# A graph stage's element-wise steps go through PSUM, its bias edge to GpSimd, and its inputs get a second buffer

## What is computed

```
# graph block
Xw = X @ Wv + bv
e = leaky_relu(Xw @ aw[:d] (as a row) + Xw @ aw[d:] (as a column) + ab, 0.2)
alpha = A * exp(e);  transition = alpha / (row sum of alpha + 1e-12)
H = sum over k = 0..2 of Xk @ Wk[k] + bk[k],  with Xk = transition @ Xk from one k to the next
return relu(H)

# ffn block: fc1, then a Mamba layer, then fc2
u, z = split(h @ W_in.T);  u = silu(causal conv of 4 taps over u + conv_b)
dt, B, C = split(u @ W_xproj.T);  delta = softplus(dt @ W_dt.T + b_dt)
state = exp(delta * A) * state + (delta * u) * B      # 1024 channels x 16 states, along the 128 positions
y = sum over the 16 states of state * C + u * D;  y = y * silu(z)
return fc2(y @ W_out.T) + b_fc2
```

## Time and profile before

| | |
|---|---|
| median of three runs | 4198.68 us |
| the profiled execution | 4201.61 us, span 4199.6 us |
| VectorE busy | 3672.1 us (87%) |
| TensorE busy (weight loads beside it) | 3628.5 us (86%) (2059.3) |
| GpSimd busy | 3444.9 us (82%) |
| ScalarE busy | 2875.8 us (68%) |
| C products (L407) | 1024 of 2355 ns |
| scans (L866) | 1024 of 2276 ns |
| state sums (L681) | 4096 products, 2036.9 us |
| decays (L460) | 4096 of 467 ns |
| transfers | 183.78 MB, 44 GB/s in the mean |
| mean granted TensorE clock | 0.947 of full speed |

### The profile page before, as it was taken

How to read it: one execution, slowest core, us unless ns; L and a number is a source line. 1 busy time by engine, 2 the same in 40 slices (tenths; PEclk the granted TensorE clock), 3 DMA queues, 4 the chain that set the end, 5 groups by cost and what they waited for, 6 DMA issues and landing times. The chain is left out here.

```text
span 4199.6 us, 44407 instructions
## 1 busy us (share of the span) xinstructions
PE 3628.5 (86%) x11386; PEld 2059.3 (49%) x11386; DVE 3672.1 (87%) x3197; ACT 2875.8 (68%) x6098; POOL 3444.9 (82%) x1828
## 2 busy tenths in 40 slices
PE   6778988888888888888888888888888888888887
PEld 3544554454554454554454554454554454554443
DVE  0399989899898999989899898998989999899998
ACT  1477667777667777667677677777667677677775
POOL 0188888988888988888888888988888888889899
PEclk9899999999999999999999999999999999999999
DMA  2111101111100111101111101111101111101110
GB/s 96 47 50 52 52 12 41 52 52 52 52 11 41 52 52 52 52 9 43 52 52 52 52 9 43 52 52 52 52 4 49 52 52 52 48 9 47 48 46 8
DMA packets 50716, 183.78 MB, mean 44 GB/s; under 512 B 7340, under 2 KB 33204, under 8 KB 42068
## 3 DMA queue, kind: packets, MB, share of 16 engines
q1 hardware_dynamic: 48880, 174.17, 10.8%
q10 hardware_dynamic: 1636, 7.83, 0.5%
HBM read 164.15 MB, written 17.83 MB: 43 GB/s over the span
## 5 line engine op out<-in xcount | busy, mean ns | idle before, releaser
L407 POOL TENSOR_TENSOR st<-st,bc 128x1024 f32<-128x1024 f32 x1024 | 2398.4, 2355 | 556.7 <-DVE st L866 365.3
L866 DVE TENSOR_TENSOR_SCAN st<-dec,st 128x1024 f32<-128x1024 f32 x1024 | 2314.5, 2276 | 83.0 <-ACT dec L460 80.5
L681 PE MATMUL y_ps<-st,ident 128*128 128x512 f32 x4096 | 2036.9, 626 | 196.0 <-POOL st L407 192.9
L460 ACT ACTIVATE dec<-delta,decay 128x254 f32<-128x254 f32 x4096 | 1696.8, 467 | 708.5 <-DVE st L866 707.1
L681 PEld LDWEIGHTS y_ps<-st,ident 128*128 128x128 f32 x4096 | 769.9, 198 | 1019.5 <-issue 576.3
L854 DVE TENSOR_TENSOR st<-du,bc 128x1024 f32<-128x1024 f32 x736 | 884.5, 1202 | 47.1 <-ACT du L446 40.3
L393 POOL TENSOR_TENSOR st<-du_sb,bc 128x1024 f32<-128x1024 f32 x288 | 678.9, 2357 | 0.1
L898 DVE SCALAR_TENSOR_TENSOR u<-d_ps,chan,u 128x250 f32<-128x250 f32 (+2 forms) x768 | 309.0, 471 | 155.6 <-ACT u L500 154.5
L677 PE MATMUL y_ps<-u,diag 128*128 128x256 f32 x512 | 170.7, 464 | 220.9 <-DVE zs L873 220.9
L701 PE MATMUL g<-wo,zs 128*128 128x256 f32 x1024 | 295.1, 440 | 0.8 <-DVE zs L873 0.8
L701 PEld LDWEIGHTS g<-wo,zs 128*128 128x128 f32 x1024 | 224.3, 222 | 104.9 <-issue 70.7
(11 more groups left out here) (106 smaller groups left out, 2698.5 us busy)
## 6 DMA issues: line engine op xcount, KB each, us to landing
bc<-bc_dram SPq DMA_DIRECT2D x64, 2048.0 KB, 9.5
xg<-x_dram SPq DMA_DIRECT2D x32, 256.0 KB, 2.8
x_dram<-xg SPq DMA_DIRECT2D x32, 256.0 KB, 2.0
last_x<-x_dram SPq DMA_DIRECT2D x32, 256.0 KB, 2.6
out_dram<-last_x SPq DMA_DIRECT2D x32, 256.0 KB, 2.2
bc<-w_inT_dram ACTq DMA_DIRECT2D x1, 4096.0 KB
adjt<-adjT_dram SPq DMA_DIRECT2D x32, 128.0 KB, 2.6
bc<-w_out_dram ACTq DMA_DIRECT2D x1, 2048.0 KB
```

The lines of the kernel that those rows point to most:

```text
L407: nc.gpsimd.tensor_tensor(st[:, sl, :, :, :], st[:, sl, :, :, :], bc[:, p, 1, SU * q:SU * q + SU, None, :].to_broadcast([P, SU, 2, T]), AL ...
L460: a = nc.scalar.activation(dec[:, v % 2, s, j, :].rearrange("p (b t) -> p b t", b=PAIR)[:, :, 1:], delta[:, p, 2 * i + j, :].rearrange("p ...
L681: mm = nc.tensor.matmul(y_all, ident[:, :], st[:, sl, s, :, :].rearrange("p j t -> p (j t)"), start=False, stop=(q == Q - 1 and s == SU - ...
L866: nc.vector.tensor_tensor_scan(h, dec[:, v % 2, :, :, :].rearrange("p s j t -> p (s j t)"), h, 0.0, ALU.mult, ALU.add).then_inc(S["scanned ...
```

## The change

The maximum and the residual go through `g0`. ScalarE writes exp(0.2 e) into the second half of the bank instead of `att2`; VectorE takes the maximum of that half and `att` into the first half, and multiplies the first half by `adjt` into `att`. The scaled sum (L967 in the changed kernel) is written back in place into `g0`, and the residual (L973) reads it there. So no VectorE instruction of the three has two inputs in SBUF. TensorE's first product of the output projection, which overwrites `g0`, now waits for `x1_made`.

The two waits of GpSimd are taken out. The bias edge is an instruction of GpSimd at step 8, behind its C product and inject, and counts a semaphore of its own (`edged`), for which the SiLU of u waits. SiLU, the projection to B, C and dt, and the softplus stand one step later each; the Ln stays at step 24.

`xg` and `adjt` get two buffers, chosen by the parity of the body. SyncE issues the loads for group k+3 at the start of body k, with waits for things of group k+1, ahead of the store of x1 of group k+2.

```diff
-X_STEPS = (11, 12)
-DT_STEPS = (14, 16, 18, 20)
-EXP_STEPS = (18, 22)
+X_STEPS = (12, 13)
+DT_STEPS = (15, 17, 19, 21)
+EXP_STEPS = (19, 23)
 LN_STEP = 24
-SILU_U, SILU_Z = 9, 3
+SILU_U, SILU_Z = 10, 3
+EDGE_STEP = 8
...
-        xg = sb("xg", [P, PAIR, DIM])
-        adjt = sb("adjt", [P, PAIR, L])
+        xg = sb("xg", [P, 2, PAIR, DIM])
+        adjt = sb("adjt", [P, 2, PAIR, L])
-        att2 = u1T[:, 0, :].rearrange("p (b i) -> p b i", b=PAIR)
...
@@ sync: body
+                g = k + 3
+                if begins and not (isinstance(g, int) and g == 0):
+                    wait(sp, "x1_stored", 16 * (g - 1))
+                    wait(sp, "normed", 2 * (g - 1))
+                    sp.dma_start(xg[:, 1 - p, :, :], x[...]).then_inc(S["x_loaded"], 16)
+                    wait(sp, "alpha_made", g - 1)
+                    sp.dma_start(adjt[:, 1 - p, :, :], adjT[...]).then_inc(S["adj_loaded"], 16)
                 if ends:
                     g = k + 2
                     wait(sp, "x1_made", g + 1)
                     sp.dma_start(x1_dram[g], xg[:, p, :, :]).then_inc(S["x1_stored"], 16)
-                g = k + 3
-                if begins and not (isinstance(g, int) and g == 0):
-                    wait(sp, "x1_stored", 16 * g)
-                    wait(sp, "normed", 2 * g)
-                    sp.dma_start(xg[:, :, :], x[...]).then_inc(S["x_loaded"], 16)
-                    wait(sp, "alpha_made", g)
-                    sp.dma_start(adjt[:, :, :], adjT[...]).then_inc(S["adj_loaded"], 16)
@@ gpsimd: body, c_product
+                        if v == EDGE_STEP:
+                            sequence_starts(pool, k + 1, r)
...
+            def sequence_starts(pool, g, r):
+                wait(pool, "taps", CONV * (g + 1))
+                first = u[:, r, :, :].rearrange("p j (b t) -> p j b t", b=PAIR)[:, :, :, 0:TAPS - 1]
+                nc.gpsimd.tensor_tensor(first, first, edge[:, :, None, :].to_broadcast([P, J, PAIR, TAPS - 1]),
+                                        ALU.add).then_inc(S["edged"], 1)
...
                 wait(pool, "scanned", U * k + v + 1)
-                for g, _, ph in steps:
-                    if ph == 13:
-                        wait(pool, "alpha_made", g + 1)
-                    if ph == 30:
-                        wait(pool, "x1_made", g + 1)
@@ scalar
                 if v == SILU_U:
-                    wait(act, "taps", CONV * (g + 1))
+                    wait(act, "edged", g + 1)
...
-                    nc.scalar.activation(att2[:, :, :], e_ps, ACT.Exp, bias=c0[:, 1:2], scale=0.2)\
+                    nc.scalar.activation(g0[:, PAIR * L:2 * PAIR * L], g0[:, 0:PAIR * L], ACT.Exp, bias=c0[:, 1:2], scale=0.2)\
@@ tensor: project_out
                         if ends:
-                            wait(pe, "h_summed", k + 4)
+                            wait(pe, "x1_made", k + 4)
@@ vector
-                if v == U_STEPS[3] + 1:
-                    wait(dve, "taps", CONV * (g + 1) - 1)
-                    nc.vector.tensor_tensor(first, first, edge[...], ALU.add).then_inc(S["taps"], 1)
...
+                    wait(dve, "aggr", 2 * g + second)
...
-                    nc.vector.tensor_tensor(att[:, :, :], att[:, :, :], att2[:, :, :], ALU.max)\
+                    nc.vector.tensor_tensor(g0[:, 0:PAIR * L], g0[:, PAIR * L:2 * PAIR * L],
+                                            att[:, :, :].rearrange("p b i -> p (b i)"), ALU.max)\
...
-                    nc.vector.tensor_tensor(att[:, :, :], att[:, :, :], adjt[:, :, :], ALU.mult)\
+                    nc.vector.tensor_tensor(att[:, :, :].rearrange("p b i -> p (b i)"), g0[:, 0:PAIR * L],
+                                            adjt[:, p, :, :].rearrange("p b i -> p (b i)"), ALU.mult)\
...
-                        a = nc.vector.scalar_tensor_tensor(x1k[:, b, :], g0[:, b * DIM:(b + 1) * DIM],
+                        a = nc.vector.scalar_tensor_tensor(g0[:, b * DIM:(b + 1) * DIM], g0[:, b * DIM:(b + 1) * DIM],
                                                            rinv[:, b:b + 1], x1k[:, b, :], ALU.mult, ALU.add)
...
-                    nc.vector.scalar_tensor_tensor(xg[:, :, :], x1k[:, :, :], 0.0, xg[:, :, :],
-                                                   ALU.max, ALU.add).then_inc(S["x1_made"], 1)
+                    x1 = xg[:, p, :, :].rearrange("p b d -> p (b d)")
+                    nc.vector.scalar_tensor_tensor(x1, g0[:, :], 0.0, x1, ALU.max, ALU.add).then_inc(S["x1_made"], 1)
```

More of the change, by code:

```diff
@@ L51 @@
 FOLD_OUT = (1, 3, 5, 7)
-CONV = (TAPS - 1) * J + 1
+EDGE_STEP = 8
+CONV = (TAPS - 1) * J
 PE_LAG = 1
@@ L355, in body @@
                     if scan:
-                        c_product(pool, k, p, v, steps)
+                        c_product(pool, k, p, v)
                         if v in POOL_DELTAS:
@@ L925, in fold_wo, with graph_dve @@
                         .then_inc(S["wo_folded"], 1)
-            def graph_dve(dve, g, v, late):
+            def graph_dve(dve, g, p, v, late):
                 if (v, late) in ((2, 0), (31, 0)):
                     second = v == 31
+                    wait(dve, "aggr", 2 * g + second)
+                    stand(dve)
                     if second:
@@ L988, in body @@
                         inject(dve, k, p, v + 1)
-                    for g, _, ph in steps:
-                        graph_dve(dve, g, ph, 0)
+                    for step in steps:
+                        graph_dve(dve, *step, 0)
                     if scan:
@@ L1000, in body @@
                         fold_wo(dve, v)
-                    for g, _, ph in steps:
-                        graph_dve(dve, g, ph, 1)
+                    for step in steps:
+                        graph_dve(dve, *step, 1)
             def tail(dve, k, p):
```

35 lines of the change are left out of this document (16 added, 19 removed).

## The result

The changed kernel takes 4124.73 us, the median of four runs from 4124.18 to 4127.08; the kernel before, on the same chip, 4199.35 (four runs). The ratio is 0.9823, with a 95% interval of 0.981 to 0.9836: 75 us less, where the prediction summed 94 and gave 4105. The profiled execution has a span of 4122.3 us.

The account below looks back on a forecast made before the run. No engine bounds throughout: VectorE is late from unit 0 to 8, GpSimd bounds units 12 to 31, TensorE is late at the jump. 13 x 4.5 + 16 x 1.8 + 7 = 94 us saved gives 4105 us; range 4085 to 4128.

Parts of the forecast that it names:

- the new wait: TensorE's output block waits for x1_made, so VectorE's gate 0 waits some 2.0 us for the state sum, some 28 times.
- X: Time from the start of TensorE's output block (L694) to the end of unit 7's state sum: 7.2 us, ends 5.6 and 11.2.
- the gain at unit 12: GpSimd's C product of unit 12 starts 1.0 us earlier per period, capped at 1.9.
- the first rival: TensorE's output block is back in time, its stretch to the sum taking 5.6 us: 120 us won, 4079 us; chance 0.17.
- The second rival: Jump period wins only what GpSimd's chain wins (4140 us), or TensorE's debt spreads (4134 us); chance 0.23.
- The 0.8 us at unit 23: GpSimd's idle 0.82 us before the C product of unit 23 goes entirely, winning 0.8 us per period.
- The jump: Where the two-body loop jumps back: gate and z products come earlier, 4.5 us won per jump period, ends 1.8 and 5.5.
- Prologue: Two graph groups lose x waits of 5.9 us each, partly covered by rstd: 7 us won for both, 0 to 11.8.
- Epilogue: End of the kernel: nothing won, as the last two bodies have no graph work.
- its later steps: ScalarE's SiLU and four dense stages one step later: costed at nothing, as ScalarE idles 35 us or more per period.
- nothing is won: Rival: the removed waits only moved, time within 0.2% of 4199 us; chance 0.05.
- the edge: Bias edge moved from VectorE to GpSimd: VectorE loses 0.2 us, GpSimd takes 0.3 us, ends 0.2 and 1.2.

Follow-up runs that it names:

- e3_onebuf: Changed kernel with one buffer of x and adj again, loads behind the store of x1 and the second norm: 4208.9 us, ratio 1.0019.
- e4_resid: Changed kernel with the scaled sum in SBUF again, TensorE's block waiting for that sum and GpSimd for the residual: 4077.05 us, ratio 0.9712.
- e2_warm: Changed kernel with eleven unread TensorE products of 256 columns in the pause ahead of the output block: 4065.58 us, ratio 0.9681.
- e9_edge_late: Changed kernel with the bias edge back on VectorE, later steps of SiLU, projection and softplus kept: 4141.85 us, ratio 0.9867.
- e6_edge: Changed kernel with the bias edge back on VectorE and SiLU, projection and softplus one step earlier again: 4199.57 us, ratio 0.9996.
- e10_before_late: Kernel before the change with only SiLU of u, projection and softplus one step later each: 4263.1 us, ratio 1.0153.
- e5_attn: Changed kernel with attention maximum and product back in SBUF, and GpSimd's wait for that product at unit 23: 4117.64 us, ratio 0.9799.
- e8_resid_warm: Changed kernel with the residual in SBUF and five unread TensorE products ahead of the output block: 4142.04 us, ratio 0.986.
- e1_out9: Changed kernel with the output projection one step later, behind the state sum of unit 7: 4079.98 us, ratio 0.9708.

## Why the prediction was right, and where it was not

- **The direction and the new wait: right.** TensorE's block took the place of the x load as what gate 0 waits for. The prediction put about 2 us some 28 times there; 2.9 to 3.8 us, 29 times, were measured. e3_onebuf shows that the second buffer, with its earlier loads, is what pays, and e4_resid that the wait for `x1_made` takes back 48 us.
- **The term that was mis-sized: X.** "I keep X = 7.2, because the clock already falls today" was wrong by 1.2 us. The clock fell before the block's first product instead of behind it, and stayed at 1.2 GHz for 5 us of the block instead of 3.4. By the prediction's own rule, the gain at unit 12 is 8.2 - X, so 1.0 becomes nothing: 29 x 1.0 = 29 us. Unit 12, 0.2 us later than before, bears this out, and e2_warm restores X = 5.6 and with it the 4079 us of the first rival, and more (4065.6). The Trainium skill, page "TensorE: Matmul & The Clock Gate", section "Part 1: The HAM clock gate (the "warmup" mystery)", says that idling throttles the array; by that rule the trace agrees (5.4 us of idling, then 0.50), and the rule spoke against this change rightly. The second rival had X = 8.2 and 4134: X came out beyond its value, the time between it and the forecast.
- **The 0.8 us at unit 23: not won in the periods without a jump.** GpSimd's gap did go. But VectorE then waited 1.3 to 1.5 us for the first decay behind the Ln, a stage that the change itself had pushed against the Ln. The prediction named it ("takes back a part of the lead") and gave it no price. It takes nearly all, and the rest went at TensorE's products behind gate 3, where the sum takes 3.62 us in a period of 124.58 us and 2.46 in one of 123.28.
- **The jump: path right, 5.1 us measured for 4.5, the size in part luck.** TensorE's pause behind gate 2 fell from 2.46 to 0.99 us and it kept its clock. But gate 2 came 2.1 us earlier and not 3, since nothing was won at unit 12, and the z products ended 3.4 us earlier (77.4 us behind the residual, not 80.8) and not 4.5. What made up for it is ScalarE's wait at the jump, which I had expected to stay and which fell from 2.93 to 1.82 (1.0 us in the mean).
- **Prologue and first period: 8.4 us for 7**, and 5.9 us more in the first period, which has no output block ahead of gate 0. **Epilogue: 3.7 us lost** for nothing forecast; body 29 has the late block and had no wait for x to lose; that this is the cause was not tested.
- **The sum:** 8.4 + 13 x 5.1 + 5.9 + 15 x 0 - 3.7 = 77 us of the span. The forecast's 94 had 1.8 for each of the 16 periods without a jump, and that is where it lost most.
- **The step that was wrong in kind: "ScalarE idles 35 us or more in a period, so I cost its later steps at nothing".** e9_edge_late against e6_edge puts them at 58 us, and e10_before_late at 68 us the other way in the kernel before. A sum of parts has no such term: what a step's place is worth depended on whether TensorE's block was late (ScalarE's wait for dbc: 4.48 or 2.75 us) and on whether there was a second buffer. The total came out near because the steps were moved in the one combination tried in which this pays; I had not seen that, so the nearness is luck to that extent.
- **A reading that was wrong: "three engines are above 87%"** in the rival "nothing is won". GpSimd is busy 107.7 of 128.6 and 107.6 of 124.0 us, which is 84 and 87%, and TensorE and VectorE lie at 88 to 92%.
- **Small prices, all near:** the edge 0.29 us (forecast 0.3), maximum and product 0.41 and 0.42 (0.47 each). The Trainium skill, page "SBUF — State Buffer", section "Who interferes with whom", says that a VectorE instruction with two SBUF inputs contends with a GpSimd instruction that reads SBUF, and one with at most one does not (outside the 2-port modes). The trace agrees: the maximum took 2.23 us with two, and takes 0.41 with one, while GpSimd works without a gap around 2003.21; with two again it takes 2.32 (e5_attn).

What stays open: why one pause of about 2 us is followed by the low clock and another of the same length at the same place is not (e8_resid_warm, 1.98 us both times). The kernel before shows it too. Its pause behind gate 2 is 2.46 or 2.47 us in both kinds of period, but the sum behind it takes 3.25 us with a jump and 1.88 without:

```profile
1936.85 1.88 PE L681 MATMUL y_ps<-st,ident 128*128 128x512 f32 x4
```

So how much of the clock kept behind gate 2 is owed to the shorter pause is not shown. In the changed kernel TensorE's pause of 1.85 us at 2033.76 is followed by a sum of 1.98 us at full clock, the pause of 2.77 us at 2042.85 by slow products. The runs changed several pauses at once, so they do not settle it. Nor does any run give the residual through the bank, alone, to the kernel before.

## What to carry to other kernels

An added wait on TensorE cost twice here: the wait, and the products behind it at half the clock. Put what others wait for ahead of the block that waits (e1_out9, 45 us), or keep TensorE busy through the pause (e2_warm, 59 us). Then look at the next pause: in e8_resid_warm the same cure made another kernel 65 us slower. Before costing a moved step at nothing, look for the instruction in which its engine waits for a third one that the same change makes late, and for the buffers whose release stands behind it. Where three engines are busy 84 to 88%, the parts of a change need not add: the later steps were worth -68, about 0 or +58 us and the second buffers 55 or 84, depending on which others were there.

## What was not expected of the hardware

- The stretch at 1.2 GHz grew with the pause at the same place in the program: 3.4 us behind 2.9 us of idling, 5 us of work behind 5.4, with one more us of it within the pause. Elsewhere the pause's length alone didn't tell it: 7 us behind 1.98 us of idling in one period, none behind the same 1.98 us in the next (e8_resid_warm).
- More work made a kernel faster: with 638 more matmul records, TensorE is busy 3666 us instead of 3598 and the kernel takes 59 us less (e2_warm).
- Once past the first periods the changed kernel repeats in a cycle of four (123.3, 123.0, 124.6, 124.1 us) although its code repeats every two; the kernel before alternates between 124.0 and 128.6.
